# Query and key rows by image of the pair, key-value head and feature: five projection units in place of six, eight masked key copies

## What is computed

```python
def local_gqa_attn(x, wq, wk, wv, wo):        # layer 1; layer 0 is the same with
    q = split_heads(x @ wq, H)                # k and v from a latent: x @ w_kv_down
    k = split_heads(x @ wk, KVH)              # H = 16 query heads, KVH = 4 kv heads
    v = split_heads(x @ wv, KVH)              # of 16 features each
    q, k = (rope(q, BASE_L), rope(k, BASE_L))
    q, k = (qk_norm(q), qk_norm(k))           # x * rsqrt(mean(x*x) + 1e-6) per head
    k, v = (repeat_kv(k), repeat_kv(v))       # four query heads share a kv head
    ...
    return merge_heads(sdpa(q, k, v, mask)) @ wo
x = x + global_latent_attn(rmsnorm(x, norm1_w), g_wq, g_kv_down, g_k_up, g_v_up, g_wo)
x = x + local_gqa_attn(rmsnorm(x, norm2_w), l_wq, l_wk, l_wv, l_wo)
```

## Time and profile before

| | us |
|---|---|
| median of 3 runs | 427.67 |
| lowest and highest | 426.64, 428.51 |
| span of the profiled execution | 425.9 |
| of it PE busy | 394.3 |
| DVE, ACT, POOL busy | 265.4, 187.7, 145.9 |
| units and attention of layer 0 | about 27 to 76 |
| units and attention of layer 1 | about 82 to 130 |
| experts | about 130 to 325 |

### The profile page before, as it was taken

One profiled execution on the slowest core, in us unless ns is written; L12 is line 12 of the kernel. 1 busy time (PEld: TensorE's weight loads), 2 busy tenths in 40 slices (PEclk: granted clock), 3 DMA queues, 4 the chain that ended last, 5 costly groups with the idle time before them and its releaser, 6 DMA issues.

```text
span 425.9 us, 8795 instructions
## 1 busy us (share of the span) xinstructions
PE 394.3 (93%) x3362; PEld 319.3 (75%) x3362; DVE 265.4 (62%) x529; ACT 187.7 (44%) x401; POOL 145.9 (34%) x119
## 2 busy tenths in 40 slices
PE   8998699898999799999999999999988999999684
PEld 6654478656786689999999999999986765567342
DVE  0368886688876875555555555555554648854776
ACT  0244832248242534444444444444435378734161
POOL 0145300363032153333333333333384246720102
PEclk9999999998999999999999999999999999999799
DMA  8930000200051022222222222232000000000001
GB/s 303 339 148 0 3 3 2 98 1 3 4 186 37 2 74 75 75 75 74 74 74 74 74 74 74 74 79 68 0 0 2 0 2 2 2 2 2 0 0 58
DMA packets 9547, 23.79 MB, mean 56 GB/s; under 512 B 1264, under 2 KB 3248, under 8 KB 9008
## 3 DMA queue, kind: packets, MB, share of 16 engines
q1 hardware_dynamic: 7632, 21.49, 15.8%
q10 hardware_dynamic: 1888, 1.93, 1.3%
HBM read 22.81 MB, written 0.61 MB: 55 GB/s over the span
## 4 chain that ended last, share of the span: by engine, by line
PE 71%; DVE 21%; issue 4%; ACT 4%; POOL 0%; DVEq 0%; ACTq 0%
PE psum L1073 70%; DVE xn L764 3%; DVE rc L838 3%; DVE nt L761 2%; DVE rn L817 1%; DVE nt L759 1%; DVE rn L816 1%; ACT region L716 1%; DVE region L839 1%; DVE xc L750 1%; DVE ra L807 1%; DVE km L1055 1%; ACT sq L532 1%; PE psum L1225 1%; DVE km L827 1%
## 5 line engine op out<-in xcount | busy, mean ns | idle before, releaser
L1073 PE MATMUL psum<-xh,split_all 128*128 128x296 f32 x544 | 122.1, 299 | 1.4 <-DVE rt L918 1.3
L431 POOL TENSOR_TENSOR split_all<-km,split_all 128x768 fp32r<-128x768 f32 x34 | 62.7, 1845 | 119.8 <-ACT split_all L645 119.8
L1073 PEld LDWEIGHTS psum<-xh,split_all 128*128 128x128 f32 x544 | 91.4, 188 | 1.9 <-DVE rt L918 1.9
L1073 PE MATMUL psum<-xl,split_all 128*128 128x296 f32 (+1 forms) x288 | 84.8, 299 | 0.0
L1073 PE MATMUL psum<-ah,split_all 128*128 128x296 f32 x272 | 73.5, 324 | 2.9 <-DVE al L981 2.4
L665 ACT ACTIVATE ah<-rt 128x296 fp32r<-128x296 f32 x68 | 30.7, 452 | 94.7 <-DVE rt L979 88.0
L1073 PEld LDWEIGHTS psum<-xl,split_all 128*128 128x128 f32 (+1 forms) x288 | 53.2, 187 | 3.2 <-issue 3.2
L976 DVE TENSOR_TENSOR rb<-ra,psum 128x296 f32<-128x296 f32 x64 | 29.6, 462 | 41.3 <-PE psum L1073 29.9
L981 DVE TENSOR_TENSOR al<-rt,ah 128x296 fp32r<-128x296 f32 x64 | 31.6, 495 | 33.2 <-ACT ah L665 33.2
L1073 PEld LDWEIGHTS psum<-ah,split_all 128*128 128x128 f32 x272 | 48.6, 192 | 4.1 <-DVE al L981 2.8
L1073 PE MATMUL psum<-al,split_all 128*128 128x296 f32 x136 | 40.6, 299 | 0.0
(11 more groups left out here) (181 smaller groups left out, 612.5 us busy)
## 6 DMA issues: line engine op xcount, KB each, us to landing
km<-in_experts SPq DMA_DIRECT2D x34, 384.0 KB, 3.0
w_sb<-in_w SPq DMA_DIRECT2D x2, 1024.0 KB, 11.8
region<-in_x SPq DMA_DIRECT2D x6, 296.0 KB, 5.5
region<-in_g_wo SPq DMA_DIRECT2D x1, 1024.0 KB, 4.8
region<-in_l_wo SPq DMA_DIRECT2D x1, 1024.0 KB, 4.8
region<-in_w_lin ACTq DMA_DIRECT2D x6, 128.0 KB, 6.7
qkv_sb<-in_qkv_w SPq DMA_DIRECT2D x1, 768.0 KB, 6.0
cst<-in_consts ACTq DMA_DIRECT2D x1, 504.5 KB, 6.8
```

What stands on the lines that cost most here:

```text
L431: nc.gpsimd.tensor_tensor(wl[i], ring[i], wh[i].bitcast(f32), ALU.subtract)\
L1073: return nc.tensor.matmul(out_, lhsT, rhs, start=start, stop=stop, skip_group_check=True)
```

## The change

The rows of a unit become (image b of the pair, kv head, feature): 2 x 4 x 16 = 128. A unit is now one query head of each group (`g` = 0 to 3) or the keys (`KEY`), for all 16 images at once: the 296 columns are the 8 pairs, and the two images of a pair are the two halves of the partitions. That makes five units, the key unit second. Each projection is written as matmuls with 64 output rows, one for b = 0 and one for b = 1. A key copy keeps one kv head of one image: eight masks over 296 columns in all. Score matmuls take the four query heads of a group along the free axis: 8 of 37 x 148 per pair. Pair p now is images 8x + t and 8x + 4 + t (x = p // 4, t = p mod 4).

```diff
-QK_UNITS = ((0, 0), (1, 0), (2, 0), (2, 1), (0, 1), (1, 1))
-ACT_VARIANTS = 4
+KEY = G4
+QK_UNITS = (0, KEY, 1, 2, 3)
+NPROJ = len(QK_UNITS)
+KEY_UNIT = QK_UNITS.index(KEY)
+PAIR_TOKENS = PAIRS * S
+VARIANTS, ACT_VARIANTS = 2 * KVH, 4
...
+        qt4 = qt[:].rearrange("p c t -> p (c t)")[:, 0:G4 * PAIR_TOKENS].rearrange("p (g t) -> p g t", g=G4)
+        km8 = km[:].rearrange("p c i t -> p (c i) t")[:, :, 0:PAIR_TOKENS]
+        kk = sq[:, 0, 0:PAIR_TOKENS]
+        def images_of(ap, b):
+            return ap.rearrange("p (x b t) -> p x b t", x=2, b=2)[:, :, b, :]
...
ACT:
-                act_e.wait_ge(s_qk, a * NPROJ + QK_UNITS.index((2, hf)) + 1)
+                act_e.wait_ge(s_qk, a * NPROJ + KEY_UNIT + 1)
...
-                    if a == 0 and u < 2:
-                        layer_norm_scale(u)
-                    if a == 0 and 1 <= u < 3:
-                        latent_copied(u - 1)
+                    if a == 0 and u == 0:
+                        layer_norm_scale(0)
+                        layer_norm_scale(1)
+                    if a == 0 and u == 1:
+                        latent_copied(0)
+                        latent_copied(1)
...
-                    if u >= 2 and QK_UNITS[u - 2][0] == 2:
-                        key_variants(a, QK_UNITS[u - 2][1])
+                    if u == KEY_UNIT + 2:
+                        key_variants(a)
...
DVE:
-                    if u >= 2 and QK_UNITS[u - 2][0] == 2:
-                        hf = QK_UNITS[u - 2][1]
-                        for g in range(ACT_VARIANTS, 8):
-                            ins = nc.vector.tensor_scalar(km[:, g // 4, g % 4, half(hf)], sq[:, 0, half(hf)],
-                                                          const("onehot8")[:, g:g + 1], None, ALU.mult)
+                    if u == KEY_UNIT + 2:
+                        for g in range(ACT_VARIANTS, VARIANTS):
+                            ins = nc.vector.tensor_scalar(km8[:, g, :], kk, const("onehot8")[:, g:g + 1], None, ALU.mult)
...
-                        dst, src = (z[:, m, half(hf)].rearrange("p (q b s) -> p q b s", b=2, s=S)
-                                    for z in ((x0, tmp)[a], x0))
-                        ins = nc.vector.tensor_tensor(
-                            dst, src, ps[4 + 2 * m + hf][:, 0:HALF].rearrange("p (b q s) -> p q b s", b=2, s=S),
-                            ALU.add)
+                        ins = nc.vector.tensor_tensor((x0, tmp)[a][:, m, half(hf)], x0[:, m, half(hf)],
+                                                      ps[4 + 2 * m + hf][:, 0:HALF], ALU.add)
...
PE:
-                        if a == 0 and 1 <= u < 3:
-                            latent_sums(u - 1)
-                        pe.wait_ge(s_xn, 2 * a + hf + 1)
+                        if u == 0:
+                            pe.wait_ge(s_xn, 2 * a + 2)
...
+                        out_ = [ps[4 + 2 * (u % 2)][64 * b:64 * b + 64, 0:HALF].rearrange("p (x t) -> p x t", x=2)
+                                for b in range(2)]
...
                             for c in range(C):
-                                w = wq_sb[a][:, c, j * P:(j + 1) * P] if j < 2 else lk_sb[:, c, :]
-                                ins = mm(bank, w, xn[:, c, half(hf)], c == 0, c == C - 1)
+                                for b in range(2):
+                                    ins = mm(out_[b], w[:, c, :], images_of(xn[:, c, 0:T], b), c == 0, c == C - 1)
+                        if a == 0 and u == 0:
+                            latent_sums(0)
+                            latent_sums(1)
...
-                for k in range(0, HALFPOS, 2):
-                    for gp in range(2):
-                        for b in range(2):
-                            cols = image(2 * p + b)
-                            out_ = ps[b0 + gp][64 * b:64 * b + S, :]
-                            ins = mm(out_[:, k * S:(k + 2) * S].rearrange("p (c s) -> p c s", c=C),
-                                     km[:, gp, k // 2, cols], qt[:, :, cols], False, True)
+                for kv in range(KVH):
+                    for b in range(2):
+                        out_ = ps[b0 + kv // 2][64 * b:64 * b + S, :]
+                        ins = mm(out_[:, kv % 2 * G4 * S:(kv % 2 + 1) * G4 * S].rearrange("p (g s) -> p g s", g=G4),
+                                 km8[:, KVH * b + kv, image(p)], qt4[:, :, image(p)], False, True)
...
-            def half_ready(a, hf):
-                pe.wait_ge(s_qk, a * NPROJ + (NPROJ // 2, NPROJ)[hf])
-                pe.wait_ge(s_km, 2 * a + hf + 1)
-                pe.wait_ge(s_kmv, 2 * a + hf + 1)
+            def keys_and_queries_ready(a):
+                pe.wait_ge(s_qk, (a + 1) * NPROJ)
+                pe.wait_ge(s_km, a + 1)
+                pe.wait_ge(s_kmv, a + 1)
```

More of the change, by code:

```diff
@@ L95, in program @@
         down_sb = sb("down_sb", [P, C, LAT])
-        gk_sb = sb("gk_sb", [LAT, P])
+        gk_sb = sb("gk_sb", [LAT, KVH * HD])
         gv_sb = sb("gv_sb", [LAT, KVH * HD])
-        lk_sb = sb("lk_sb", [P, C, P])
+        lk_sb = sb("lk_sb", [P, C, KVH * HD])
         lv_sb = sb("lv_sb", [P, C, KVH * HD])
@@ L553, in key_variants @@
                 for g in range(ACT_VARIANTS):
-                    ins = nc.scalar.activation(km[:, g // 4, g % 4, half(hf)], sq[:, 0, half(hf)], ACT.Copy,
-                                               scale=const("onehot8")[:, g:g + 1])
+                    ins = nc.scalar.activation(km8[:, g, :], kk, ACT.Copy, scale=const("onehot8")[:, g:g + 1])
                 ins.then_inc(s_km, 1)
@@ L1111, in qk_units @@
                     if u < NPROJ:
-                        j, hf = QK_UNITS[u]
-                        if a == 0 and 1 <= u < 3:
-                            latent_sums(u - 1)
-                        pe.wait_ge(s_xn, 2 * a + hf + 1)
-                        if a == 0 and j == 2:
-                            pe.wait_ge(s_latv, hf + 1)
+                        j = QK_UNITS[u]
+                        if u == 0:
+                            pe.wait_ge(s_xn, 2 * a + 2)
+                        if a == 0 and j == KEY:
+                            pe.wait_ge(s_latv, 2)
                         if u >= 2:
                             pe.wait_ge(s_rope, n - 1)
-                        bank = ps[4 + 2 * (u % 2)][:, 0:HALF]
-                        if j == 2 and a == 0:
-                            ins = mm(bank, gk_sb[:], latent[:, half(hf)], True, True)
+                        out_ = [ps[4 + 2 * (u % 2)][64 * b:64 * b + 64, 0:HALF].rearrange("p (x t) -> p x t", x=2)
+                                for b in range(2)]
+                        if j == KEY and a == 0:
+                            for b in range(2):
+                                ins = mm(out_[b], gk_sb[:], images_of(latent[:, 0:T], b), True, True)
                         else:
+                            w = lk_sb if j == KEY else wq_sb[a][:, :, j * 64:(j + 1) * 64]
                             for c in range(C):
-                                w = wq_sb[a][:, c, j * P:(j + 1) * P] if j < 2 else lk_sb[:, c, :]
-                                ins = mm(bank, w, xn[:, c, half(hf)], c == 0, c == C - 1)
+                                for b in range(2):
+                                    ins = mm(out_[b], w[:, c, :], images_of(xn[:, c, 0:T], b), c == 0, c == C - 1)
                         ins.then_inc(s_proj, 1)
+                        if a == 0 and u == 0:
+                            latent_sums(0)
+                            latent_sums(1)
                     if u >= 1:
@@ L1198, in grouped_values @@
                             const("pair_ones", ROWS)
-                        ex = e[0:ROWS, p % 2, 0:EC].rearrange("p (g n) -> p g n", g=2)
-                        ins = mm(ps[p % 2][VP * kv:VP * (kv + 1), part * G4 * S:(part + 1) * G4 * S]
-                                 .rearrange("p (g n) -> p g n", g=2),
-                                 w, ex[:, :, kv * 2 * S:(kv + 1) * 2 * S], True, True)
+                        ins = mm(ps[p % 2][VP * kv:VP * (kv + 1), part * G4 * S:(part + 1) * G4 * S],
+                                 w, e[0:ROWS, p % 2, kv * G4 * S:(kv + 1) * G4 * S], True, True)
                 ins.then_inc(s_o, 1)
@@ L1261, in attention @@
                         pe.wait_ge(s_v, 6)
-                    if a < 2 and p == PAIRS // 2:
-                        half_ready(a, 1)
                     if 0 <= p - lead < PAIRS:
@@ L1323, in _ @@
                 pe.wait_ge(s_rope, NPROJ * (a + 1))
-                half_ready(a, 0)
+                keys_and_queries_ready(a)
                 attention(a)
@@ L1572, in layouts @@
     a["vecs"] = v
-    c, gp, kv, d = np.meshgrid(np.arange(C), np.arange(2), np.arange(KVH), np.arange(HD), indexing="ij")
-    q_col = ((kv * 4 + 2 * c + gp) * HD + d).reshape(-1)
-    k_col = (kv * HD + d)[0].reshape(-1)
+    g, kv, d = np.meshgrid(np.arange(G4), np.arange(KVH), np.arange(HD), indexing="ij")
+    q_col = ((kv * G4 + g) * HD + d).reshape(-1)
     def by_group(w):
```

(4 more changed lines are left out.)

14 lines of the change are left out of this document (7 added, 7 removed).

## The result

| | us |
|---|---|
| kernel before, median of 4 runs | 428.00 (426.64 to 428.51) |
| kernel after, median of 4 runs | 432.18 (430.82 to 433.71) |
| ratio after / before | 1.0106, 95% interval 1.0074 to 1.0139 |
| span of the profiled execution, before and after | 425.9 and 430.9 |

The change makes the kernel 1.1% slower, 4.2 us by the medians and 5.0 us by the spans. The prediction was 431.8.

The account below looks back on a forecast made before the run. PE has 71% of the chain of waits, DVE 21%; the start of values(0) decides in each layer. Full-clock terms +0.1 and +0.2, clock +2.1 and +1.7, make +4.1 us: 431.8 us, range 427.0 to 434.8.

Parts of the forecast that it names:

- The point to follow: Start of values(0) in layers 0 and 1: what happens to it passes through nearly whole to the end.
- The front: First projections wait for both halves of `xn`: layer 1 starts at 84.17, 1.8 us later; layer 0 at about 28.9.
- The turn and the copies saved: Units: five instead of six and one key-copy set less; last query 2.8 us earlier in layer 0, 2.5 in layer 1.
- the same three units or two follow now, with one set: DVE from the compared `rb` to the last query's write: 14.63 us in layer 0, 11.53 in layer 1.
- rival (b): DVE's chain is shorter than carried over, up to 4.0 us in both layers: 425.0 us; chance 0.10.
- The wait that moves: Scores(0) and scores(1) come behind the last query: 2.95 us for two pairs, with 0.07 gained a pair.
- The clock: PE's clock falls in the gap before the scores: +2.1 us in layer 0, +1.7 in layer 1, 0 for the fronts.
- (d): The fronts of both layers lose the clock as well: 1.3 us on each, up to 434.4 us; chance 0.14.
- The reading that no gap of this size matters: PE's idle gaps ahead of the scores do not lower the clock: the sum would be +0.3 us.
- (a): Clock holds at both attention starts or drops beside the path: 428.0 us, no measurable change; chance 0.22.
- (c): The 64-row projections do not overlap: PE has 1.0 us more per unit, about 437 us; chance 0.04.

Follow-up runs that it names:

- all fillers: Kernel after with unused matmuls added in PE's four long gaps, ahead of the first projections and of the wait for the last query: 426.73 us, ratio 0.9969.
- The kernel before with this wait alone: Kernel before with one wait moved, every projection waiting for both halves of the normalised stream: 434.91 us, ratio 1.0176.

## Why the prediction was right

**The point to follow.** It said that the start of values(0) decides in each layer and passes through nearly whole. The 5.46 us at layer 1's values(0) are 5.43 at the last values and 5.46 behind the experts.

**The front.** The first projections were forecast at about 28.9 and at 84.17. Layer 0's is at 28.83. Layer 1's is at 83.48 with all fillers, where layer 0 is 0.68 ahead of before (51.58 against 52.26), and 83.48 + 0.68 = 84.16. The kernel before with this wait alone shows the cost.

**The turn and the copies saved.** At full clock the last query was forecast at 49.3 in layer 0 and is at 48.46 with fillers, 0.8 earlier. The step that was off is "the same three units or two follow now, with one set": it carried DVE's turns over (3.09 and 2.96 in layer 0), and they fell to 2.46 and 2.48, 1.1 less; against this the last turn, with the second set of copies gone, gave back 0.95 and not 1.21. Part of rival (b) came true. Its reason was nearly right: L821 is long where POOL's operation has started first, and not whenever POOL works. In layer 1, from the first projection to the last query, the forecast was 103.0 - 84.2 = 18.8 and the measurement 18.8.

**The wait that moves.** 2.95 + 0.1 behind the last query forecast, 3.12 measured at full clock, since a pair gains 0.02 and not 0.07. At full clock the forecast had values(0) of layer 1 0.3 later than before, and with fillers it is 0.5 earlier: the 0.8 from DVE's turns. The median with fillers is 1.5 below before, and so is the profiled execution; the other 1.0 of that execution arises in the feed-forward block.

**The clock.** This was the whole of the loss, and its terms were 2.1 and 1.7 with nothing for the fronts. Measured in the profiled execution: 2.54 on layer 0's scores, 1.56 on layer 1's and 1.68 on layer 0's front. The first was under-sized, the second over-sized, and the front's, kept for the range as (d), came in layer 0 and not in layer 1. Values(0) of layer 0 starts at 55.81 where 54.5 was forecast for a low clock: 1.7 from the front and 0.4 from the scores, less DVE's 0.8. That the sum of 4.1 hit 4.2 is in part luck. By values(0) of layer 1 the loss is 5.46: 2.0 more of clock than forecast (5.8 against 3.8), and 0.1 where layer 0's low stretch runs on past values(0), less DVE's 0.8. The spans differ by 5.0, and the medians by 4.2. The reading that no gap of this size matters would have given 428.0.

**The rivals.** (a) falls by the rows at 0.50. (c) falls by 1.22 against 2.21 for a projection.

## What to carry over

When work is merged into fewer, later-finishing units, look for what ran in the shadow of the last unit: a consumer that could start on the first half now waits for all, and that can eat all that the merging saves. Then look at the gap that the wait opens ahead of dense PE work, since the clock may be at half when the work comes; fillers there were worth 5.4 us, and real work moved into the gap 3.1 us more. And order the new units so that part of the consumer can go early: here two of four query heads.

## What the runs showed of the hardware

- Where the clock's low stretches fall differs from run to run. Seven of the ten variants had one of 3.4 us in the experts, between 138 and 156 us, and before, after and three variants with fillers had none; from values(0) of layer 1 to the copy of the experts' sum are 219.5 us with it (105.38 to 324.88 with all fillers) and without (105.86 to 325.35 before), so it lies beside the path.
- The kernel before ranges over 2 to 4 us without any change. Its runs at a mean granted clock of 0.991 or more took 426.6 to 428.1, and those at 0.980 or less 428.2 to 430.5.
- A turn of PE longer by 0.12 us made the whole faster, some 1.2 us of it because two operations on DVE and POOL changed their order. DVE's L821 is 0.47 where it starts alone or ahead of POOL's multiplication, and 0.95 to 1.09 where that started first.
- Two matmul chains to different output halves of the array overlap even if one is queued entirely ahead of the other: 1.23 us for both, against 2.21 in one half.
